# Differential attention block: pairs of sub-heads instead of groups of four

## The reference

```python
q = (x @ Wq).reshape(B, S, 2 * H, d).transpose(0, 2, 1, 3) * scaling
k = (x @ Wk).reshape(B, S, 2 * H, d).transpose(0, 2, 1, 3)
v = (x @ Wv).reshape(B, S, H, 2 * d).transpose(0, 2, 1, 3)
scores = jnp.einsum('bhqd,bhkd->bhqk', q, k)
scores = jnp.where(causal_mask, -jnp.inf, scores)
probs = jax.nn.softmax(scores, axis=-1).reshape(B, H, 2, S, S)
attn = jnp.einsum('bhqk,bhkd->bhqd', probs[:, :, 0] - lam * probs[:, :, 1], v)
attn = attn * lax.rsqrt(jnp.mean(attn * attn, -1, keepdims=True) + RMS_EPS) * rms_w * (1.0 - LAMBDA_INIT)
x = _layernorm(x + attn.transpose(0, 2, 1, 3).reshape(B, S, H * 2 * d) @ Wo)
r = sigmoid(xr @ W_r.T); k = xk @ W_k.T      # xr, xk mix x with the token before it
x = _layernorm(x + r * (jnp.square(relu(k)) @ W_v.T))
```

## Time and profile before

| | us |
|---|---|
| median of 3 runs | 461.19 |
| the profiled execution | 459.95 |
| its span | 458.2 |
| PE busy | 396.4 (87%) |
| DVE busy | 382.1 (83%) |
| ACT busy | 347.3 (76%) |
| POOL busy | 199.4 (44%) |

### The profile page before, as it was taken

How to read it: one execution, slowest core, us unless ns; L and a number is a source line. 1 busy time by engine, 2 the same in 40 slices (tenths; PEclk the granted TensorE clock), 3 DMA queues, 4 the chain that set the end, 5 groups by cost and what they waited for, 6 DMA issues and landing times.

```text
span 458.2 us, 14401 instructions
## 1 busy us (share of the span) xinstructions
PE 396.4 (87%) x5191; PEld 167.3 (37%) x5191; DVE 382.1 (83%) x504; ACT 347.3 (76%) x687; POOL 199.4 (44%) x356
## 2 busy tenths in 40 slices
PE   5355669999999999999999999999999999899582
PEld 3241313343334333333333343433333434345452
DVE  2459998999999999999999999999999992334643
ACT  3360047989898999899998989898989998767333
POOL 7200011245555453637373646455554535553312
PEclk9795557999999999999999999999999999999877
DMA  5589020203030211212030202030202010000001
GB/s 135 207 303 340 23 93 2 97 1 95 4 94 6 91 43 50 54 39 93 0 93 0 93 0 93 0 93 1 92 10 83 1 49 3 1 0 24 24 1 46
DMA packets 20363, 28.40 MB, mean 62 GB/s; under 512 B 3936, under 2 KB 8928, under 8 KB 20208
## 3 DMA queue, kind: packets, MB, share of 16 engines
q1 hardware_dynamic: 19664, 27.44, 18.7%
q10 hardware_dynamic: 672, 0.59, 0.4%
HBM read 20.39 MB, written 9.47 MB: 65 GB/s over the span
## 4 chain that ended last, share of the span: by engine, by line
PE 46%; DVE 26%; ACT 13%; issue 11%; ACTq 2%; DMA 1%; POOL 1%; DVEq 0%; POOLq 0%
DVE part_max L1013 22%; PE acc L615 16%; ACT e_buf L924 10%; PE mx L530 9%; PE ex L584 7%; PE ex L627 2%; PE ex L646 1%; PE mx L615 1%; PE mx L712 1%; DMA x_tok<-in_L_attn_x 1%; PE mx L713 1%; ACTq L285 1%; PE mx L697 1%; PE mx L732 1%; DVE rest L973 1%
## 5 line engine op out<-in xcount | busy, mean ns | idle before, releaser
L924 ACT ACTIVATE e_buf<-ex 128x512 f32<-128x512 f32 x576 | 305.7, 599 | 44.8 <-PE ex L584 38.6
L1013 DVE TENSOR_REDUCE part_max<-mx 128x2 f32<-128x1024 f32 (+2 forms) x288 | 330.7, 1209 | 8.6 <-PE mx L530 7.3
L615 PE MATMUL acc<-e_buf,v_grp 128*32 128x256 f32 (+2 forms) x2200 | 177.6, 395 | 3.0 <-issue 2.8
L584 PE MATMUL ex<-qe,ke 26*128 26x512 bf16 (+3 forms) x768 | 145.4, 334 | 1.8 <-ACT e_buf L924 0.2
L530 PE MATMUL mx<-km,qm 29*128 29x128 bf16 (+3 forms) x1280 | 118.9, 273 | 23.1 <-DVE part_max L1013 21.1
L456 POOL TENSOR_SCALAR_AFFINE_SELECT e_buf<-e_buf 128x512 f32<-128x512 f32 x128 | 78.9, 635 | 131.0 <-ACT e_buf L924 131.0
L530 PEld LDWEIGHTS mx<-km,qm 26*128 26x128 bf16 (+1 forms) x1280 | 41.8, 94 | 145.6 <-DVE part_max L1013 135.9
L615 PEld LDWEIGHTS acc<-e_buf,v_grp 128*32 128x32 f32 x2200 | 43.7, 108 | 57.4 <-issue 51.6
L584 PEld LDWEIGHTS ex<-qe,ke 26*128 26x128 bf16 x768 | 44.3, 91 | 28.0 <-ACT e_buf L924 17.9
L440 POOL TENSOR_TENSOR r_rms<-sq_eps,minus_half 128x16 f32<-128x16 f32 x15 | 43.7, 2911 | 1.2
L419 POOL TENSOR_TENSOR r_lam<-r_den,lam_pair 128x32 f32<-128x32 f32 x15 | 4.0, 266 | 64.6 <-DVE r_den L1059 64.6
(11 more groups left out here) (134 smaller groups left out, 261.9 us busy)
## 6 DMA issues: line engine op xcount, KB each, us to landing
qm<-q_rows SPq DMA_DIRECT2D x16, 256.0 KB, 2.7
km<-k_rows SPq DMA_DIRECT2D x16, 256.0 KB, 2.9
qe<-q_rows SPq DMA_DIRECT2D x16, 256.0 KB, 3.1
ke<-k_rows SPq DMA_DIRECT2D x16, 256.0 KB, 3.3
q_rows<-part_q SPq DMA_DIRECT2D x6, 256.0 KB, 5.0
k_rows<-part_k SPq DMA_DIRECT2D x6, 256.0 KB, 4.9
q_rows<-part_q SPq DMA_DIRECT2D x6, 192.0 KB
k_rows<-part_k SPq DMA_DIRECT2D x6, 192.0 KB
```

What stands on the lines that cost most here:

```text
L584: scored = pe.matmul(ex[:, ex_slot(b, i) % EX_BANKS, col:col + w], ke[par][rows, P * kb:P * (kb + 1)], qe[par][rows, q1 - w:q1], start=col ...
L615: last = pe.matmul(bank[STRIP * j:STRIP * (j + 1), hi - w:hi], v_grp[par][:, kb, j // 2, shift:shift + STRIP], e_buf[:, k % ESLOTS, j, col ...
L924: nc.scalar.activation(e_buf[:, k % ESLOTS, 2 * p + i, :], ex[:, ex_slot(b, i) % EX_BANKS, :], ACT.Exp).then_inc(s["exped"], 1)
L1013: nc.vector.tensor_reduce(target, mx[m % 2][:].rearrange("p s (a b) -> p s a b", a=a), AX.X, ALU.max).then_inc(s["maxed"], 1)
```

## The change

The unit of the program is a pair of sub-heads (`PAIR` = 2), of which there are 32 (`NPAIR`); a group of four is now two pairs, `pr` = 0 and 1, and stays the unit for values, normalisation and placement.

- A pair has 9 maxima units and 9 bursts; a burst scores both sub-heads of one whole quad. `EARLY` stays 8, so the exponentials are 9 + 8 = 17 units behind the maxima. Maxima rows lie on partitions 64 to 127, exponential rows on 0 to 63, and each row load is 64 rows. `e_buf` holds a whole pair (9 slots of 2 x 512 columns), and each exponential waits for the sum of the pair before in its slot.
- The sums of 512 queries of two sub-heads are cut into two pairs of blocks, (0, 3) and (1, 2) (`BLOCKS_OF`, `sum_pieces`), so that they still fill four strips, of 256 columns (`HALF`). A step is 4 matmuls of 256 columns, 6 of 128 and 256, or 8 of 128.
- The copies and transposes of sums and maxima come once per pair, at b = 3, 6 and 4, with half the columns.
- The split of the maxima moves from VectorE to GpSimd (`split_maxima`), behind the masks of quad 1.
- `load_max_rows` and `load_exp_rows` read 64 rows (`q_pair`, `k_pair`), `place_maxima` 16 rows of `max_rows` at a time.
- `normalise` is cut: the power and the placement (`place_attn`, now four instructions) of group g-2 stand in pair 0, the rest for group g-1 in pair 1.
- The first batch's work moves into the last group's two pairs, and the last pair alone is summed in halves: the first half is taken at burst 7 and stored at burst 8 of 9. VectorE's order at the end changes.

```diff
-NU = 2 * len(MAX_UNITS)
+NU = len(MAX_UNITS)
...
+BLOCKS_OF = [(0, 3), (1, 2)]
...
+def sum_pieces(k):
+
+
+    pieces = []
+    for c, kb, col, w in QUADS[k]:
+        first = 4 - w // P
+        for ab, own in enumerate(BLOCKS_OF):
+            blocks = [q for q in own if q >= first]
+            if blocks:
+                cols = [col + P * (q - first) for q in blocks]
+                pieces.append((c, kb, ab, 2 - len(blocks), cols))
+    return pieces
...
-TAKE_AT, TURN_AT, MAXIMA_AT, INVERT_AT = 3, 6, 13, 9
...
+TAKE_AT, TURN_AT, MAXIMA_AT, INVERT_AT = 3, 6, 4, 1
...
-            sp.dma_start(qe[par][:], q_group[n]).then_inc(s_qke[par], 16)
...
+            def pair(n, pr, g):
+                if not isinstance(n, int) or n + 2 < NPAIR:
+                    load_max_rows(sp, n + 2, pr)
+                if not isinstance(n, int) or n + 1 < NPAIR:
+                    load_exp_rows(sp, n + 1, 1 - pr)
+                    place_maxima(sp, n + 1, 1 - pr, g + pr)
...
+            def place_attn(n):
+
+                wait(pool, s["norm_steps"], 9 * n + 8)
                 pool.tensor_tensor(r_rms[:], sq_eps[:], minus_half[:], ALU.pow).then_inc(s["norm_steps"], 1)
 
-                pool.wait_ge(s["norm_steps"], steps * n + 9).then_inc(s["norm_seen"], 1)
...
-                        .then_inc(s["attn_ready"], 1)
-
-            def group(n, par):
-                last = isinstance(n, int) and n == NG - 1
+                    for ab in range(2):
+                        pool.tensor_tensor(attn_out(n, c, ab), attn_chunks[:, c, ab], r_rms_chunks[:, c, ab],
+                                           ALU.mult).then_inc(s["attn_ready"], 1)
+
+            def split_maxima(n):
+
+                if not isinstance(n, int) or n > 0:
+                    pool.wait_ge(s["max_turned"], n)
+                pool.wait_ge(s["combined"], n + 1).then_inc(s["maxima_seen"], 1)
+                pool.tensor_copy(turn_max[:, 0], row_max[:]).then_inc(s["max_high"], 1)
+                pool.wait_ge(s["max_high"], n + 1).then_inc(s["maxima_seen"], 1)
+                pool.tensor_tensor(turn_max[:, 1], row_max[:], turn_max[:, 0], ALU.subtract)\
+                    .then_inc(s["max_split"], 1)
...
+                    if k == 1 and not (isinstance(g, int) and n + 1 >= NPAIR):
+                        split_maxima(n + 1)
+                    if (pr, k) == (0, 2) and not (isinstance(g, int) and g < 2):
+                        place_attn(g - 2)
+                    if (pr, k) == (1, 2) and not (isinstance(g, int) and g + 1 >= NG):
+                        stage_values(g + 1, 1 - par)
...
-                        normalise(n - 1, 1 - par)
+                    if (pr, k) == (1, 2) and not (isinstance(g, int) and g == 0):
+                        normalise(g - 1, 1 - par)
+                    if (pr, k) == (1, 2) and isinstance(g, int) and g == NG - 1:
+                        place_attn(g - 1)
...
+            def sum_burst(g, par, pr, k):
+
+                n = 2 * g + pr
+                alone = isinstance(n, int) and n == NPAIR - 1
+                if k == 0:
+                    pe.wait_ge(s["v_grp_set"], g + 1)
...
+                pe.wait_ge(s["exped"], 2 * NQ * n + 2 * k + 2)
+                if DIAG[k]:
+                    pe.wait_ge(s["masked"], NSEL * n + SEL_BY[k])
+                for c, kb, ab, i, cols in sum_pieces(k):
+                    over = k == NQ - 1 or (alone and c == 0 and k == FIRST_HALF - 1)
+                    bank = last_acc if alone and c == 1 else acc[:, 0:HALF]
+                    shift = 0 if c == 1 else VPAD
+                    first = k == 0 or (alone and c == 1 and k == FIRST_HALF - 1)
+                    for jj in range(PAIR):
+                        strip = slice(STRIP * (2 * jj + ab), STRIP * (2 * jj + ab + 1))
+                        v = v_grp[par][:, kb, pr, shift:shift + STRIP]
+                        if len(cols) == 2 and cols[1] != cols[0] + P:
+                            out = bank[strip, :].rearrange("p (a t) -> p a t", t=P)
+                            e = e_buf[:, k, jj, :].rearrange("p (a t) -> p a t", t=P)[:, 0:4:3, :]
+                        else:
+                            out = bank[strip, P * i:HALF]
+                            e = e_buf[:, k, jj, cols[0]:cols[-1] + P]
+                        last = pe.matmul(out, v, e, start=first, stop=over, skip_group_check=True)
...
-            beside = {(NG - 2, 14): [(turn_attn, 0), (turn_attn, 1)], (NG - 2, 16): [(project, 0), (project, 1)],
-                      (NG - 1, 3): [(turn_x1, 0)], (NG - 1, 5): [(ffn_k, 0)],
-                      (NG - 1, 7): [(ffn_r, 0), (turn_x1, 1)], (NG - 1, 9): [(ffn_k, 1), (ffn_o, 0)],
-                      (NG - 1, 11): [(ffn_r, 1)], (NG - 1, 17): [(ffn_o, 1)]}
-
-            def group(n, par):
-
-                static = isinstance(n, int)
-                for b in range(NB2):
+            beside = {(0, 1): [(turn_attn, 0)], (0, 2): [(turn_attn, 1)], (0, 3): [(project, 0)],
+                      (0, 4): [(project, 1)], (0, 8): [(turn_x1, 0)], (1, 0): [(ffn_k, 0)], (1, 1): [(turn_x1, 1)],
+                      (1, 2): [(ffn_r, 0)], (1, 3): [(ffn_k, 1)], (1, 4): [(ffn_o, 0)], (1, 5): [(ffn_r, 1)],
+                      (1, 7): [(ffn_o, 1)]}
...
-                    for own, h in SUMS_AT[b]:
-                        if own == 0:
-                            sum_half(n, par, h)
-                        elif not (static and n == 0):
-                            sum_half(n - 1, 1 - par, h)
-                    if b == 12 and static and n == NG - 1:
-                        turn_sums(NG, par, acc[:])
-                    if static:
-                        for stage, ch in beside.get((n, b), []):
+                        turn_sums(n, 1 - pr, ex[:, SUMS_SLOT % EX_BANKS, 0:HALF])
+                    if b >= LAG:
+                        sum_burst(g, par, pr, b - LAG)
+                    elif not (static and n == 0):
+                        sum_burst(prev[0], par if pr == 1 else 1 - par, 1 - pr, NQ - LAG + b)
+                    if b == NQ - 1 and static and n == NPAIR - 1:
+                        turn_sums(NPAIR, pr, acc[:, 0:HALF])
+                    if static and g == NG - 1:
...
-            beside = {(NG - 2, 14): [(copy_attn, 0), (copy_attn, 1)], (NG - 1, 4): [(copy_x1, 0)],
-                      (NG - 1, 6): [(relu_k, 0)], (NG - 1, 8): [(gate_r, 0), (copy_x1, 1)],
-                      (NG - 1, 10): [(relu_k, 1)], (NG - 1, 12): [(gate_r, 1)]}
...
+            beside = {(0, 1): [(copy_attn, 0)], (0, 2): [(copy_attn, 1)], (0, 8): [(copy_x1, 0)], (1, 1): [(relu_k, 0)],
+                      (1, 2): [(copy_x1, 1)], (1, 3): [(gate_r, 0)], (1, 4): [(relu_k, 1)], (1, 6): [(gate_r, 1)]}
...
+                for b in range(NQ):
+                    if not (static and n == 0):
+                        act.wait_ge(s["summed"], NQ * (n - 1) + b + 1)
+                    for i in range(PAIR):
                         if (b, i) == (TAKE_AT, 1) and not (static and n == 0):
...
-                        store_sums(n - 1, 1 - par, ex[:, SUMS_SLOT % EX_BANKS, :])
-                    if b == MAXIMA_AT and not (static and n + 1 >= NG):
-                        copy_maxima(n + 1, MAXIMA_SLOT % EX_BANKS)
...
+                    if b == 7 and static and n == NPAIR - 1:
                         take_half(0)
-                    if b == 13 and static and n == NG - 1:
+                    if b == 8 and static and n == NPAIR - 1:
                         store_half(0)
-                    if static:
...
-                    if m == NU:
-                        split_high(n + 1)
-                    if m == NU + 1:
-                        split_low(n + 1)
...
             norm_attn(0)
+            norm_attn(1)
             apply1(0)
-            norm_attn(1)
             apply1(1)
             invert(NG - 2, 0)
             square_k(0)
             norm_ffn(0)
+            square_k(1)
+            normalise_half(0)
+            norm_ffn(1)
+            place_half(0)
             apply2(0)
-            normalise_half(0)
-            square_k(1)
-            place_half(0)
```

406 lines of the change are left out of this document (194 added, 212 removed).

## The result

| | before | after |
|---|---|---|
| median of 20 executions each, us | 461.21 (457.38 to 464.35) | 463.52 (461.21 to 466.16) |
| ratio, 95% interval | | 1.0062 (1.0033 to 1.0092) |
| profiled execution, us (span, mean granted clock) | 459.95 (458.2, 0.934) | 463.57 (461.8, 0.934) |

The kernel became 0.6% slower where 2.4% faster was predicted; 463.52 lies above the range.

What follows compares the result with a forecast made beforehand. VectorE's reduces were taken as the bound, PE close behind. From the profiled 459.95 us: -7.7 + 3.1 - 9.1 - 1.6 + 4.8 - 0.5 + 1.2 = 450.2, predicted 450; own range 446 to 455, eight in ten 440 to 461.

Steps and rivals of the forecast that it cites:

- What bounds the kernel: VectorE's 288 reduces bound 32.9 to 379.1 us, unless PE is held up in one burst beyond its lead.
- the 0.10 taken: VectorE's gap at each of 31 turning bursts, taken as 0.10 us between bounds 0 and 0.44: +3.1 us.
- the second rival: Turning burst's old gap returns in every pair, 31 x 0.44 = 13.6 us instead of 3.1: 460.7, no change; chance 0.17.
- The walk: Bursts 3 to 8 of a pair: PE's maxima units reach VectorE with 0.05 to 0.7 us to spare.
- The fixed cost of small copies: ScalarE's 47 more PSUM copies: 6.7 us, counted only if ScalarE were the bound.
- VectorE's small work: Cast and subtraction leave VectorE (2.4 us in 16 groups); combine comes 32 times at 0.18 us, 5.8 against 4.0.
- The term of -7.7: VectorE's whole stream, 338.5 us after against 346.2 in the trace, without the turning bursts' idle time.
- Distance: Exponentials 17 units behind the maxima, not 26: nine bursts fewer after the last maximum, -9.1 us; PE's chunk 0 wait goes, -1.6.
- The end: Last sum steps queue on PE behind chunk 2's transposes, 7.4 us against 2.6: +4.8; narrower copies and transposes behind: -0.5.
- The +1.2 of the clock: After PE's idle wait at the end, steps 7, 8 and the transposes fall into the low-clock spell: +1.2 us.
- The stream's end: VectorE's reduces, beginning near 32.9 us, were to end near 374 us.
- The third rival: Row loads come later than PE wants them, costing 31 x the delay; from 0.5 us on 466; chance 0.11.

Runs made afterwards that it cites:

- b1: Kernel before the change, each VectorE reduce reading 896 of its 1024 columns; 449.24 us, one execution.
- b2: Kernel before the change, each exponential shortened to 448 of 512 columns; 458.66 us, one execution.
- r4: Changed kernel, ScalarE's banks numbered over four pairs, both transposes sharing one bank, sum step ahead of them; 453.10 us, one execution.
- f1: Changed kernel, PE's sum step put ahead of the transposes of maxima and of sums; 463.87 us, ratio to before 1.0076.
- h1: g1 with the cast and subtraction of each pair's maxima put back from GpSimd on VectorE; 455.42 us, ratio to before 0.9860.
- s4: Changed kernel, the cast and subtraction of each pair's maxima put back from GpSimd on VectorE; 463.60 us, ratio to before 1.0049.
- b3: Kernel before the change, exponentials following the maxima by 30 units instead of 26 (EARLY 12 for 8); 464.50 us, ratio 1.0102.
- e1: Changed kernel, last two sum steps and second half's transposes put ahead of chunk 2's transposes at the end; 460.14 us, ratio to before 1.0001.
- f2: f1 with each VectorE reduce reading 896 of 1024 columns; 463.09 us, one execution.
- r1: Changed kernel, ScalarE's three PSUM banks numbered over a ring of four pairs; 466.22 us, ratio to before 1.0114.
- r2: r1 with the transposed sums and transposed maxima sharing one bank; 459.07 us, ratio to before 0.9948.
- g1: r4 and e1 together on the changed kernel; 450.76 us, ratio to before 0.9778.

## Why the prediction was wrong

*What bounds the kernel.* Right for before (b1 gains, b2 does not), by 0.8 us in 21.6. The step that failed is the one behind it: "VectorE decides unless PE is held up in one burst by more than its lead". Only single bursts were held against VectorE; the loop of PE and ScalarE was never summed over a whole pair. Summed, one group of before has eighteen bursts and one passage, at most 20.85 us, and the changed one two passages, 22.19: above VectorE's 21.3. The loss of 0.43 us a pair (31 x 0.33 more than the 0.10 taken, 10.2 us) is that excess. r4, which leaves VectorE's work as it is and moves only where PE and ScalarE meet, gives 0.30 of it back. It is the second rival that came about, in size (0.44 a pair; it said 460.7 us) and in a part of its cause: it named PE's bank waits on ScalarE in two places of a pair. It too took them for gaps of single bursts; f1 removes the wait before the transposes, and the period stays.

*The walk* over bursts 3 to 8 gave burst 4 rightly (1.68 for 1.70), but began with PE a full unit ahead, 1.12 us; in the pair shown it is 0.98 (203.46 to VectorE's 204.44). From burst 4 to burst 7 it has 4.08 us where the trace has 4.25 (burst 6 is 1.24 in the walk, 1.55 in the trace, and 1.51 in the prediction's own count). These 0.3 us use up the margin of 0.05 and give the step of 1.41 at 208.14. In a loop that is longer than VectorE's period PE does not regain its lead. A walk must close on itself after one period.

*The fixed cost of small copies.* The prediction set 6.7 us for 47 more ScalarE copies aside, to count "only if ScalarE were the bound". After, ScalarE's part of the loop is in the bound, so the reason for leaving them out is gone. How much of the excess is the copies' own time no run shows: r4 has as many of them, and its period is 10.78. The copy of the sums at half the columns lasts 0.37 us, 0.58 before, so half the columns save 0.21 and 0.16 stay:

```profile
203.37 0.37 ACT L901 COPY o_rows<-acc 128x256 f32<-128x256 f32 x1
```

By the Trainium skill ("VectorE: DVE Perf Modes", section on the TRN2 errata) a ScalarE instruction that reads PSUM pays 172 cycles beside its columns, which makes (172 + 256) / 1.2 GHz = 0.36 us; the trace agrees.

*VectorE's small work.* The combine was mis-sized: 0.33 us in the stream of after (a step of 1.46 instead of 1.13), not 0.18, 32 times: 4.8 us. Its listed duration is 0.22. The prediction counted from the end of one reduce to the start of the next (0.50 for combine and reciprocal); from start to start, as the stream runs, the two cost 0.58 in before (a step of 1.71) and 0.33 and 0.27 in after. So half the elements took 0.07 off the duration (0.29) and nothing off the price in the stream. The term of -7.7 also counts as saved the 0.5 us by which its own list (345.7) falls short of the trace (346.2). The split's 2.4 us were sized about right (h1: 0.17 us a pair), but in after they buy nothing (s4).

*Distance.* Right: the first exponential at 52.17 (about 52 said), the last 31.8 us after the last reduce (32), 72.7 us from that reduce to the end of the span (74.0 by its terms: 79.2 - 9.1 - 1.6 + 4.8 - 0.5 + 1.2); b3 gives 4.7 us for four units at the first exponential. PE's wait of the earlier trace rows before the transposes of x1 is gone from after's trace.

*The end.* Right: PE waits 4.40 us (about 4), and e1 takes back 3.4 us in the medians, 5.0 in the profile. The +1.2 of the clock came too: behind that wait the transposes take 1.12 us (0.66 in e1) and the twenty matmuls of the sum steps 1.94, where e1 has 36 in 2.03.

*The stream's end* at 374 became 389. Gaps 10.2 and combines 4.8 us make the 15, and less the 1.3 us by which the rest came out shorter they are about the 13.4 between 450.15 and the profiled 463.57.

*Row loads.* The third rival is refuted: the trace of after has one wait for a load of rows, 0.4 us ahead of a weight load at 88.97. GpSimd's 235 us busy hid as said, in after; with the sum step moved ahead they no longer do (f2).

## What to carry to other kernels

Where three engines alternate through a few buffers, sum the loop over one whole period beside the busiest engine's stream; a second line 4% below the bound is the next bound. A change that makes a unit of work smaller repeats every fixed passage (copy, transpose, handover of a buffer) and must be charged for it on the loop in which it lies, not on the engine that it relieves. And where two engines wait for each other, moving one wait shows nothing until the place at which they meet again is mended too: f1, r1 and r2 looked like small or no gains, r4 was worth 10 us.

## What the runs showed of the hardware

A reduce of 1024 PSUM columns lasts 1.22 us but follows its neighbour after 1.131. A small reduce of 0.22 between two of them costs the stream 0.33 us and two in a row 0.38; a reciprocal of 0.34 costs 0.27; a cast of 0.19 costs 0.06 in before, and up to 0.27 in h1.

The time of one and the same program moves with the mean clock that it is granted. The executions of before beside f1 have spans of 455.3 to 456.0 us at a mean granted clock of 0.941, 458.2 to 458.8 at 0.934 and 461.4 to 462.3 at 0.923 to 0.926. Every kept trace has 1.00 from 80 to 380 us; what differs lies ahead of that and behind it. Ten us behind the last exponential of e1 and of g1 (PE, PEld, DVE, ACT, POOL busy, granted clock, DMA):

```profile
431.00:441.00 10.00, 7.31 (x34) 5.60 (x35) 4.92 (x26) 4.01 (x10) 2.48 (x4) 0.69 0.09 26
```

```profile
421.00:431.00 10.00, 6.71 (x20) 4.42 (x21) 4.85 (x27) 2.72 (x6) 2.49 (x4) 0.50 0.09 26
```

The same work, 10 to 20 us behind the last exponential, at 0.69 on the mean and at 0.50, the lower level (1.2 GHz) throughout; PE had waited for VectorE (2.48 us) shortly before in both. So g1's end is 3 us longer than e1's with the same program there, and one of g1's six executions, at a mean clock of 0.948, took 446.7 us. A gain of a few us in such a stretch can be seen in the trace, and not in a single time.
